# Macaron block (expert layer, attention, expert layer): low halves of the expert weights subtracted from a PSUM copy of the high halves

## The reference, cut to what matters

```python
x = x + 0.5 * ffn(layernorm(x))
x = x + attention(layernorm(x))
x = x + 0.5 * ffn(layernorm(x))        # the same weights as the first time

def ffn(x):                            # 16 experts, two of them for each row, and one shared by all rows
    probs = softmax(x @ Wr.T + bias)
    w, idx = top_k(probs, 2); w = w / (sum(w) + 1e-9)
    y_e = (silu(x @ Wg[e]) * (x @ Wu[e])) @ Wd[e]          # 256 -> 128 -> 256
    shared = (silu(x @ sWg) * (x @ sWu)) @ sWd
    return sum_over_the_two(w * y_e) + shared
```

## Time and profile before

| what | us |
|---|---|
| three timed runs, median (lowest, highest) | 349.83 (349.80, 351.58) |
| span of the profiled execution | 375.8 |
| profiled execution, time beside its span | none is given; its span is 26.0 above the median |
| PE busy in the span | 276.6 (74%) |
| DVE busy | 244.9 (65%) |
| ACT busy | 167.1 (44%) |
| POOL busy | 130.5 (35%) |
| the 17 `wl` (L1212), first to last start | 15.9 to 52.2 |
| first product of the expert loop | 57.4 |

### The profile page before, as it was taken

The page is one execution under the profiler, slowest core; times in us unless marked ns, Lnnn a source line. Parts: engine busy times, 40 slices in busy tenths (PEclk is TensorE's granted clock), DMA queues, the critical chain, the costliest instruction groups (busy, mean ns, idle before and its releaser), DMA issues.

```text
span 375.8 us, 6430 instructions
## 1 busy us (share of the span) xinstructions
PE 276.6 (74%) x1911; PEld 199.4 (53%) x1911; DVE 244.9 (65%) x800; ACT 167.1 (44%) x433; POOL 130.5 (35%) x181
## 2 busy tenths in 40 slices
PE   1747649888882587989999999987384598898710
PEld 1537428877771254555444444654273287787700
DVE  8686865757666871658888885466841266667616
ACT  3566604434443155357666666662321044444300
POOL 7027841555456003300445200000077125555630
PEclk9966757999997799898999999999696599999965
DMA  7996654434400617980534400000022603344127
GB/s 249 385 388 191 261 161 161 120 99 130 131 19 15 210 42 185 197 250 26 113 88 85 86 3 1 2 3 0 0 101 98 195 15 110 108 138 131 31 81 254
DMA packets 29861, 45.69 MB, mean 122 GB/s; under 512 B 5323, under 2 KB 22961, under 8 KB 29444
## 3 DMA queue, kind: packets, MB, share of 16 engines
q1 hardware_dynamic: 24164, 33.41, 29.2%
q0 software_dynamic: 5664, 11.87, 10.9%
HBM read 27.98 MB, written 20.61 MB: 129 GB/s over the span
## 4 chain that ended last, share of the span: by engine, by line
PE 54%; DVE 19%; issue 7%; DMA 7%; ACT 7%; POOL 2%; another core or an unknown queue 2%; SPq 1%; POOLq 0%; DVEq 0%; ACTq 0%
PE bank L313 23%; PE bank L1015 5%; PE bank L1054 5%; PE bank L1028 4%; PE bank L320 4%; PE bank L947 4%; PE bank L871 3%; DVE wl L1212 3%; DMA yg<-results 2%; DVE res L1384 2%; PE bank L1032 2%; DMA stk_q<-parts_d 1%; DVE xn L1227 1%; PE bank L856 1%
## 5 line engine op out<-in xcount | busy, mean ns | idle before, releaser
L568 POOL DMA_INDIRECT results<-ysb,xp x62 | 61.5, 993 | 75.4 <-DVE ysb L1351 55.6
L1440 DVE CUSTOM_DVE_ANT_0 bank<-bank,dec 128x512 f32<-128x512 f32 (+3 forms) x128 | 59.8, 518 | 18.2 <-PE bank L1015 18.0
L1312 DVE TENSOR_TENSOR hm<-sg,bank 128x128 f32<-128x128 f32 x78 | 22.3, 286 | 51.4 <-ACT sg L654 30.7
L820 ACT ACTIVATE ct<-bank 128x512 f32<-128x512 f32 (+1 forms) x96 | 45.0, 520 | 22.0 <-PE bank L1032 21.9
L654 ACT ACTIVATE sg<-bank 128x128 f32<-128x128 f32 x78 | 21.5, 276 | 63.8 <-PE bank L313 54.4
L557 POOL DMA_INDIRECT slots_x<-xn,slot x32 | 34.1, 1064 | 33.3 <-DVE slot L1289 24.3
L313 PE MATMUL bank<-wh,xT_h 128*128 x124 | 41.3, 333 | 3.7 <-DVE xT_l L1339 2.9
L700 ACT ACTIVATE xT_h<-bank 128x256 fp32r<-128x256 f32 x62 | 23.8, 386 | 34.7 <-PE bank L947 30.6
L871 PE MATMUL bank<-ident,hm 128*128 128x128 f32 x78 | 23.7, 304 | 20.4 <-issue 11.3
L1015 PE MATMUL bank<-stk_q,stk_k 96*128 96x512 bf16 (+3 forms) x128 | 34.9, 310 | 2.1 <-DMA stk_q<-parts_d 1.8
L313 PE MATMUL bank<-wh,hT_h 128*128 (+1 forms) x78 | 30.7, 394 | 7.2 <-issue 2.7
(11 more groups left out here) (186 smaller groups left out, 681.5 us busy)
## 6 DMA issues: line engine op xcount, KB each, us to landing
xp<-slots_x SPq DMA_DIRECT2D x30, 257.0 KB
w_raw<-in_experts SPq DMA_DIRECT2D x17, 384.0 KB, 8.4
yg<-results SPq DMA_DIRECT2D x16, 256.0 KB, 4.8
slots_x<-zeros SPq DMA_DIRECT2D x2, 1285.0 KB, 11.8
parts_d<-part SPq DMA_DIRECT2D x6, 384.0 KB, 3.2
stk_k<-parts_d SPq DMA_DIRECT2D x8, 192.0 KB, 3.8
stk_q<-parts_d POOLq DMA_DIRECT2D x8, 192.0 KB, 4.9
slots_x<-zeros SPq DMA_DIRECT2D x1, 1413.5 KB, 7.8
```

Of the source, the lines that this page charges most:

```text
L568: pool.indirect_dma_start(results, where, ysb[c % RING][:], None, bounds_check=4 * N - 1, oob_is_err=False).then_inc(s_ys[c % RING], 16)
L820: act.activation(ct[n % 6][:, a:b], bank[2 + i][:, 0:b - a], ACT.Exp).then_inc(s_exp, 1)
L1440: dve.tensor_tensor_reduce(s_i, s_i, dec[:, SEQ - w:SEQ], 1.0, NEG, ALU.add, ALU.max, mmax[g % 2][:, n % G * QT + i:n % G * QT + i + 1])\
```

## The change

TensorE multiplies the high half of each of the 16 routed experts by an identity (`ident_r`, new, in float32r) into two banks, 384 columns each: `show_high(q)`. DVE's subtraction reads that copy from PSUM in place of `wh` from SBUF, in two pieces (`split_low_beside`). The pairs of banks alternate: (0, 1) for odd q, (6, 7) for even q. `show_high(q)` waits for the low half of q-2, which frees the pair. Since banks 6 and 7 are taken so in `ffn(0)`, the shared expert's `down` writes there into bank 4 or 5, the bank that held the transpose of the same tile; `hidden_turn` of two tiles later waits until DVE has added that result to `res`. On DVE the addition moves ahead of `hidden_low`, in both layers. POOL makes `ident_r` (one more copy of 128x128 at the start).

```diff
@@ POOL, start
+            link(pool.tensor_copy(ident_r[:], ident[:]))
@@ PE
-            def down(j, par, wd):
+            def down(j, par, wd, to=6):
                 pe.wait_ge(s_htl, j + 1)
-                three(pe, bank[6 + par][:, 0:D], ...
+                three(pe, bank[to + par][:, 0:D], ...
@@ PE, ffn
+                def show_high(q):
+                    pe.wait_ge(s_whi, q + 1)
+                    if q > 2:
+                        pe.wait_ge(s_wlo_v, q - 1)
+                    for c in range(2):
+                        mm = pe.matmul(bank[wh_bank[q % 2][c]][:, 0:WP], ident_r[:],
+                                       wh[:, order[q], c * WP:(c + 1) * WP], start=True, stop=True,
+                                       skip_group_check=True)
+                    mm.then_inc(s_whp, 1)
+
+                if f == 0:
+                    show_high(1)
...
                     if i < NT:
                         gate_up(j, j % 2, f == 0 and i < 2, rows(i), w_s)
                     if 0 <= i - 1 < NT:
+                        if f == 0 and i >= 3:
+                            pe.wait_ge(s_ysh, i - 2)
                         hidden_turn(j - 1, (j - 1) % 2, f == 0 and i - 1 < 2)
                     if 0 <= i - 2 < NT:
-                        if i - 2 >= 2:
+                        if f and i - 2 >= 2:
                             pe.wait_ge(s_ysh, f * NT + i - 3)
-                        down(j - 2, j % 2, lambda b: (wh, wl)[b][:, E, KT * GU:WE])
+                        down(j - 2, j % 2, lambda b: (wh, wl)[b][:, E, KT * GU:WE], 6 if f else 4)
+                    if f == 0:
+                        for q in (i + 2,) if i < 6 else (2 * i - 4, 2 * i - 3):
+                            show_high(q)
+                if f == 0:
+                    show_high(E)
@@ DVE
+            def split_low_beside(q):
+                e = order[q]
+                for c in range(2):
+                    part = slice(c * WP, (c + 1) * WP)
+                    if c == 0:
+                        dve.wait_ge(s_whp, q)
+                    ins = dve.tensor_tensor(wl[:, e, part], w_raw[:, e, part], bank[wh_bank[q % 2][c]][:, 0:WP],
+                                            ALU.subtract)
+                ins.then_inc(s_wlo_v, 1)
@@ DVE, ffn
+                    if 0 <= i - 3 < NT:
+                        dve.wait_ge(s_y, j - 2)
+                        y = bank[(6 if f else 4) + (j - 3) % 2][:, 0:D]
+                        dve.scalar_tensor_tensor(out=res[:, i - 3, :], in0=y, ...).then_inc(s_ysh, 1)
                     if 0 <= i - 1 < NT:
                         hidden_low(j - 1, (j - 1) % 2)
-                    if 0 <= i - 3 < NT:
-                        ...
                     if f == 0:
                         for q in (i + 1,) if i < 6 else (2 * i - 5, 2 * i - 4):
-                            split_low(q)
+                            split_low_beside(q)
```

More of the change, by code:

```diff
@@ L154, in macaron_kernel @@
         big = sb("big", [P, NB * E], F32, r2)
-        iota_i = sb("iota_i", [P, 512], I32, r2)
+        iota_i = sb("iota_i", [P, 512 - P], I32, r2)
+        ident_r = sb("ident_r", [P, P], F32R, r2)
         mx = sb("mx", [P, NT], F32, r2)
@@ L208, in macaron_kernel @@
         s_wlo_v = sem("s_wlo_v")
+        s_whp = sem("s_whp")
         s_rw = sem("s_rw")
@@ L296, in macaron_kernel @@
         EARLY = 8
+        wh_bank = ((6, 7), (0, 1))
+        WP = WE // 2
         NJ = NT + NB
@@ L871, in hidden_turn @@
                 pe.transpose(bank[4 + par][:, 0:P], hm[par][:], ident[:]).then_inc(s_ht, 1)
-            def down(j, par, wd):
+            def down(j, par, wd, to=6):
                 pe.wait_ge(s_htl, j + 1)
-                three(pe, bank[6 + par][:, 0:D], lambda k, a: hT[par][a][:], lambda k, b: wd(b),
+                three(pe, bank[to + par][:, 0:D], lambda k, a: hT[par][a][:], lambda k, b: wd(b),
                       [(0, 0, 0), (0, 0, 1), (0, 1, 0)]).then_inc(s_y, 1)
@@ L1324, in ffn @@
                         times_up(j, j % 2, f == 0 and i < 2)
+                    if 0 <= i - 3 < NT:
+                        dve.wait_ge(s_y, j - 2)
+                        y = bank[(6 if f else 4) + (j - 3) % 2][:, 0:D]
+                        dve.scalar_tensor_tensor(out=res[:, i - 3, :], in0=y, scalar=0.5, in1=res[:, i - 3, :],
+                                                 op0=ALU.mult, op1=ALU.add).then_inc(s_ysh, 1)
                     if 0 <= i - 1 < NT:
                         hidden_low(j - 1, (j - 1) % 2)
-                    if 0 <= i - 3 < NT:
-                        dve.wait_ge(s_y, j - 2)
-                        dve.scalar_tensor_tensor(out=res[:, i - 3, :], in0=bank[6 + (j - 3) % 2][:, 0:D], scalar=0.5,
-                                                 in1=res[:, i - 3, :], op0=ALU.mult, op1=ALU.add).then_inc(s_ysh, 1)
                     if f == 0:
                         for q in (i + 1,) if i < 6 else (2 * i - 5, 2 * i - 4):
-                            split_low(q)
+                            split_low_beside(q)
                 def step(b, live):
```

## The result

The changed kernel took 356.53 us (median of four runs, 353.73 to 360.52) against 349.81 for the kernel before on the same chip: 1.0182 of it, 95% interval 1.0114 to 1.0251. Six more runs, taken with the experiments, gave 356.80 and a ratio of 1.0133, 1.0058 to 1.0207. The medians hold all runs; the ratios leave out those in a slow state, such as the 360.52. The change costs 1.3 to 1.8% by the two ratios, some 5 to 6 us, with intervals from 0.6 to 2.5%, and the forecast of 356.2 stands.

What follows compares the result with a forecast made beforehand. DVE's low halves behind 41 us in the first expert layer were taken as the bound. Low halves 7.1 us later less 0.9 from the clock (+6.2), plus 0.2 for the second layer, on 349.83 gave 356.2 us; range 351.7 to 361.5.

Steps and rivals of the forecast that it cites:

- The ring: First expert layer, from pass 3: PE's transpose waits for DVE's res, DVE's hT_l for transpose and ACT's copy.
- One turn: One round of the ring, from gate_up to show_high: 3.92 us at half clock, 2.73 at full.
- The pass from hm(6) to hm(7): First layer, show_high(9) ahead of gate_up(7) waits for a low half: 5.25 us at half clock, 4.3 at full.
- the tail from hm(7): First layer, DVE's work from hm(7) to the end of the last low half: 11.4 us.
- two of the three turns at full, the rest at half, and the start in the middle: Clock assumed for the ring in the first layer: last low half ends at 60.3 us, 7.1 behind.
- the full-clock rival: TensorE at 2.4 GHz from 30 us on: last low half 4.4 us late, 351.5 us in all; chance 0.14.
- the 2.9 us that the clock was to give back: Six idle products and first three gate_ups of the expert loop at full clock: up to 2.9 us, 0.9 counted.
- The subtraction: DVE's low half from PSUM in two pieces: 0.07 us more each, 0.8 over the 11 behind 40 us.
- The copies on PE: Each show_high, two products: 0.64 us at half clock, 0.36 at full; all 16 take 10.2 or 5.8.
- POOL: First layer: row copies all at 0.20 us, excesses of 3.1 us gone, slot loads at about 48.3, not 51.45.
- The faster case: Rival: POOL and clock freed, ring covered by other DVE work: -2.8 us, 347.0; chance 0.08.
- The second layer: res ahead of hT_l there costs 0.33 us a pass, 0 to 2.6 in all; +0.2 counted.

Runs made afterwards that it cites:

- e3: The kernel before plus the 32 copy products on PE, written to banks 0 and 1 that nobody reads: 349.83 us, 0.9984.
- e1b: Repeat, unedited, of the changed kernel with results back in banks 6 and 7, DVE's old order and copies through banks 0 and 1: 353.9 us, 1.0078.
- e8: e1 with banks 2 and 3 as a second pair for the copies from the tenth low half on: 351.97 us, 1.0035.
- e0: The kernel before, unedited, profiled a second time: 349.28 us.
- e7: The kernel before with ten more filler products on PE behind the last shared result: 349.35 us, 0.9955.
- e1: The changed kernel with results back in banks 6 and 7, DVE's old order and copies through banks 0 and 1: 352.9 us, 1.0054.

## Why the prediction was right

*The ring: right, and shown.* The two idle times that it named came where it named them (0.73 in front of hT_l, forecast some 0.8; PE released by res), the ring alone makes a loss of that size, and the changed kernel without it loses 0.5 to 0.8%. One turn was forecast at 2.73 us at full clock and measured 2.77; at half clock without the copies the same sum makes 3.92 - 0.64 = 3.28, and the run with the ring alone shows 3.42; at full clock it makes 2.73 - 0.36 = 2.37, and that run's first turn shows 2.43. The pass from hm(6) to hm(7) took 4.36 and 5.04 (bounds 4.3 and 5.25), the tail from hm(7) 11.57 and 11.69 (11.4).

*The step that was mis-sized: "two of the three turns at full, the rest at half, and the start in the middle".* All three turns were at full clock in both profiles, and hm(3) came at 33.8, the full-clock value of 33.7. So the low halves ended at 58.05 and 58.80, near the 57.5 of the full-clock rival and not at 60.3. That rival's time of 351.5 was wrong all the same, for two reasons. "Against about 53.15 before" took the end from one profile, whose span was 26 us above the median; in the second it is 51.78, so the full-clock path is 5.7 us late and not 4.4. And the 2.9 us that the clock was to give back weren't there: on the fillers it was 2.72 - 1.46 = 1.26 in one profile and nothing in the other. The 1.65 of the gate_ups were the kernel before's already: in its second profile the clock behind the fillers is 0.82, not the 0.50 of the earlier trace rows. The errors cancel, and that they do is luck: the turns were put 2 us too long, the kernel before 1.4 us too late. The forecast of +7.1 for the low halves met 6.3 and 7.0, but with less insight into the clock than the agreement suggests.

*The subtraction: right.* A low half from PSUM takes 1.01 us alone against 0.95, and 0.97 against 0.91 in a stream of two (1.94 and 1.82): 0.06 more, forecast 0.07. The price of the Trainium skill's page "VectorE: DVE Perf Modes" (the errata for TRN2), by an estimate from its figures 0.19 more for each, isn't borne out by these rows.

*The copies on PE: 0.35 for a pair at full clock (0.36 forecast).* Unread, they change nothing (e3). Read outside the ring, they come with 0.35 to 0.8% more time, of which at most 16 x 0.06 = 1.0 us is the subtraction, 0.1 us (full clock) to 0.4 us (half) for each low half of the tail the two banks, and 0.64 a pass the copies themselves where the clock is half and PE sets the pace (e1b). How much each holds in the median stays open, because clock and late loads differ between the profiles.

*POOL: right, and worth nothing here.* Copies at 0.20, slots loaded at 48.57 (forecast 48.3); against the second profile of the kernel before, 50.01, that is 1.4 us sooner and not 3.1. With the same ring but SBUF operands the copies took up to 0.94. That agrees with the rule in the Trainium skill's "SBUF — State Buffer" (who interferes with whom). The faster case failed where the prediction placed it: DVE has nothing else to take while it waits.

*The second layer: +0.2 was small enough.* PE's fillers there are released by the scatters' landing (the 283.52 row), not by res; its new order isn't on the path. From the first product of the first layer's expert loop to these fillers the changed kernel takes 283.52 - 60.84 = 222.68 us and the kernel before, in its second profile, 279.17 - 56.05 = 223.12, so no loss was made there. The order was not tried alone.

## What to carry to other kernels

Before two results share a bank, write down who must answer whom in one pass: if the bank's release stands behind the next product's consumer on an in-order engine, buffers that decoupled two engines become a ring, and its turn is the sum of both. Offloading an operand costs little here (0.06 us for the subtraction, 0.35 us for a pair of copies); the bank that it needs cost 1.6% when it was taken alone. And take the baseline's landmarks from more than one profile: here they differ by 1.4 us between two profiles of one kernel.

## What the runs showed of the hardware

- The granted clock did not follow the work in one stretch alone. With copies read outside the ring it was 0.97 from 47 to 53 and 0.50 from 53 to 58 (e8). In the kernel before it was 0.50 and then 0.82 (e0), with fillers 0.68 and then 1.00 (e7), with the unread copies 0.77 and then 0.50 (e3). In two of the three changed runs the later stretch had the half clock, in one the full. In three of the first four runs of the changed kernel a higher mean clock went with a shorter time (0.890: 353.73, 0.878: 355.03, 0.872: 358.04).
- Weight loads that share the DMA engines with POOL's scatters (DMA share 1.02 and 0.98 from 34.65 to 41.48) took different times to land in two executions of the same kernel: 6.0 to 8.3 us from issue for the last six loads in e1, 4.0 to 5.9 in e1b. ACT stood up to 3.64 us for one of them in e1 and for none in e1b's shared passes. The ring hides this: in the changed kernel, where they took 4.0 to 7.3 us, no wait of ACT for one of them shows.
